# Flamingo block: the first chunk of x transposed ahead of its scale, Newton's step split between two engines, and GpSimd's order in the attention's last step

## The chip, the cores and the metric

The kernel runs on one core of one Trainium2 chip. A core has a matrix engine (TensorE, PE in the profile), a vector engine (VectorE, DVE), a scalar engine (ScalarE, ACT), GpSimd (POOL), and SyncE (SP), which only issues DMAs here. The metric is device time in microseconds, the median of several executions.

## The reference

Eight sequences of 256 rows of 256 numbers pass through a gated cross-attention with 16 heads and a gated feed-forward network whose activations and weights are rounded to 8 bits:

```python
x = x + tanh(g_xattn) * xattn(layernorm(x), ctx, ctx, Wq, Wk, Wv, Wo, bo, masks)
x = x + tanh(g_ffn) * ffn(layernorm(x), clip_x, clip_down, w_gate, w_up, w_down)

def act_fake_quant(x, clip):            # one scale for the whole tensor
    scale = sigmoid(clip) * max(abs(x)) / 127
    return clip_to_8_bits(round(x / scale)) * scale

def ffn(x, ...):
    xq = act_fake_quant(x, clip_x)
    h = act_fake_quant(silu(xq @ q(w_gate).T) * (xq @ q(w_up).T), clip_down)
    return h @ q(w_down).T
```

Two layer norms need a mean and 1/sqrt(variance + 1e-5) of each row. The scale of xq needs the largest magnitude of the whole normalised tensor, so no product of the feed-forward can begin before the last row is normalised.

## The kernel before

A batch is one sequence: 256 rows, two tiles of 128 partitions. There are B = 8 batches, 16 tiles, and every engine has a program of its own; semaphores order them. Each engine does its instructions in the order in which they are written.

**Projections.** For each batch VectorE takes row statistics (`stats`, L915 and L919), GpSimd turns the variance into 1/sqrt (`project_rstd`, `rstd`, L499 to L506), VectorE normalises (`normalise`, L925), TensorE transposes x and the context (`x_tr`, L1303 and L1309), ScalarE and VectorE copy the transposes, and TensorE projects (L1345, L1356). q and k are split into three bf16 parts by ScalarE (L702, L711), VectorE (L940) and GpSimd (`lo_parts`, L516); SyncE stores them in DRAM (L435) and loads them back stacked. The part buffers are two, by the batch's parity: batch 2's first parts wait until batch 0's have landed. SyncE's queue is one list: `ctx_load` of batch b (L352) waits until TensorE has transposed the context of batch b - 2; behind `ctx_load(3)` stand the loads of the feed-forward weights and the small inputs, and behind those the store of batch 0's parts.

**1/sqrt.** `rstd` is six operations of GpSimd over two columns: add epsilon (L499), raise to the power -0.5 (L500), and one Newton step in four operations (L501 to L506), which mends the rough power. Before the first of them GpSimd writes two rows of ones into k_st with a memset of 4096 words on two partitions (L492) and waits for it.

**Attention.** A step works on batch b while the maxima of batch b + 1 are taken. GpSimd's part of a step: the split of the maxima, the hats of an earlier batch (`hat`, L563 and L567: the second layer norm, written into v_all), head scales, `residual` (L576), `add_bias` (L589), `second_rstd`. VectorE takes the statistics of the second norm (L1070, L1078) and the row maxima of the hats (`row_maxima`, L1083). After the last step GpSimd works off what is left: residuals, one `rstd` over four columns for batches 4 and 5 at once (`newton_two`), the hats of batches 4 and 5, `second_rstd` and `hat` of batch 6, and `second_rstd` of batch 7. VectorE's `last_step` closes with the row maxima of batch 6, the residual of batch 7 (L1064) and its statistics; `last_row_maxima` (L1090, L1093) subtracts the mean of batch 7 and takes its maxima, and ScalarE multiplies these rows by rs2 (L850).

**From the attention to the feed-forward.** VectorE multiplies batch 7's maxima by rs2 (L1185), reduces, TensorE spreads the maximum over the partitions (L1545), VectorE makes the scale (L1189 to L1191). x comes in four chunks of 512 rows. For chunk 0, VectorE and ScalarE each scale half of it to int8 (L1203, L882), VectorE casts both halves to bf16 (L1195), TensorE transposes each half (L1573), ScalarE copies the transposes (L858), and TensorE multiplies, half by half (`first_product`, L1591). Chunks 1 to 3 are scaled by VectorE (1) and GpSimd (2 and 3, `over_scale`, L648, after a wait for the casts of chunk 0), cast by VectorE, and transposed between products. GpSimd's memset L643 pads h_all before that. wd_scale and PALL come from a product and a spread of TensorE (L1549, L1545) that VectorE reads.

Of the kernel before, what the change touches and what calls it, by code (L numbers as in the profile page):

```python
# [21 lines left out]
P = 128  # L22
# [43 lines left out]
def flamingo_block(nc, x, ctx_in, mask_rows, mask_full, g_xattn, g_ffn, Wq, Wk, Wv, Wo, bo,  # L66
# [60 lines left out]
    with ExitStack() as stack:  # L127
# [38 lines left out]
        minus_half = sb("minus_half", [P, 2, QC])  # L166
        newton_two = sb("newton_two", [P, 3, 2, QC])
        stats2 = sb("stats2", [P, QC, 6])
        mv2_now = sb("mv2_now", [P, 2, QC, 2])
        rs2 = sb("rs2", [P, NT])  # L170
        row_max = sb("row_max", [P, NT])
# [49 lines left out]
        x_int = part(NCH * CT * E // 4, True).bitcast(I8).rearrange("p (a t e) -> p a t e", a=NCH, t=CT)  # L221
        xq_b = part(NCH * CT * E // 2).bitcast(BF16).rearrange("p (a t e) -> p a t e", a=NCH, t=CT)
# [60 lines left out]
        poison_sum, x_over_scale, last_hat = sem("poison_sum"), sem("x_over_scale"), sem("last_hat")  # L283
        xq_ready, xq_tr, xq_t_ready = sem("xq_ready"), sem("xq_tr"), sem("xq_t_ready")
# [194 lines left out]
        def _(pool):  # L479
# [7 lines left out]
            chain.step(pool.memset(minus_half[:].rearrange("p a c -> p (a c)"), -0.5))  # L487
# [4 lines left out]
            pool.memset(k_st[KR:KM].rearrange("r a h s -> r (a h s)").bitcast(mybir.dt.uint32), 0x3F803F80  # L492
                        ).then_inc(ones_rows, 1)
            pool.wait_ge(ones_rows, 1)

            def rstd(y, var, v, t, out, half=minus_half[:, 0]):
# [3 lines left out]
                chain.step(pool.tensor_tensor(y, v, half, ALU.pow))  # L500
# [5 lines left out]
                return pool.tensor_tensor(out, y, t, ALU.mult)  # L506

# [15 lines left out]
            for b in range(3):  # L523
                project_rstd(b, b % 2)
# [109 lines left out]
            rstd(newton_two[:, 2], mv2_now[:, :, :, 1], newton_two[:, 0], newton_two[:, 1],  # L634
                 rs2[:, QC * (B - 4):QC * (B - 2)].rearrange("p (a c) -> p a c", a=2), minus_half[:]).then_inc(rs2_ready, 2)
# [17 lines left out]
            pool.wait_ge(xq_ready, 2)  # L653
# [19 lines left out]
        def _(act):  # L673
# [170 lines left out]

            act.activation(scal[:, 21:22], magic[:], ACT.Silu)
# [8 lines left out]
            def first_xq_copy(half):  # L854

                act.wait_ge(xq_tr, half + 1)
                cols = slice(half * 2 * P, (half + 1) * 2 * P)
                act.activation(xq_t[:, :, cols], spare[half][:].bitcast(BF16).rearrange("p (k t) -> p k t", k=EC)[:, :, cols],  # L858
                               ACT.Copy).then_inc(xq_t_ready, 1)

            def xq_copy(n):
                act.wait_ge(xq_tr, n + 2)
# [37 lines left out]
        def _(dve):  # L900
# [9 lines left out]
            def stats(b, p, j):  # L910
# [9 lines left out]
                done.then_inc(stats_done, 1)  # L920

# [49 lines left out]
            stats(0, 0, 0)  # L971
            normalise(0, 0)
# [205 lines left out]
            dve.wait_ge(diag_done, 1)  # L1178
            chain.step(dve.tensor_reduce(PALL, bank_o[:, E:E + P], axis=AX.X, op=ALU.add))
            chain.then(dve.tensor_tensor(SIG[:, 0:1], SIG[:, 0:1], PALL, ALU.add))  # L1180
            dve.tensor_copy(wd_scale[:], bank_o[:, 0:E]).then_inc(wd_scale_ready, 1)
            dve.wait_ge(rs2_ready, B + 1)
            dve.wait_ge(row_done, B)
# [490 lines left out]
```

## Time and profile before

| | us |
|---|---|
| median of 3 runs | 248.92 (248.47 to 249.05) |
| the profiled execution | 250.41 |
| its span | 248.8 |
| PE busy | 210.6 (85%) |
| DVE busy | 207.0 (83%) |
| ACT busy | 160.5 (64%) |
| POOL busy | 133.3 (54%) |

The span counts from the first to the last instruction; 1.6 us lie around it. A busy share is an average over stages with different limits. What a change is worth is read in its own stage: which wait ends last there. A timeline row merges neighbouring instructions of one kind (x2 is two of them) and closes with the idle time before it and what ended that. Line numbers are those of the kernel before.

### The profile page before, as it was taken

Reading aid. Unit: us, or ns where it says so; the run is one execution under the profiler, and the core shown is the slowest. Engines: PE = TensorE matmul, PEld = TensorE weight load, DVE = VectorE, ACT = ScalarE, POOL = GpSimd, SP = SyncE. Lnnn points to the kernel's source line nnn. Section 1 sums busy time; section 2 is a strip of 40 time slices with the busy share of each in tenths; the row PEclk is TensorE's granted clock in tenths of the full one; section 3 lists DMA queues with packets and bytes.
Section 4 is the critical chain, followed back from the end, with each engine's and each line's share of the span. In section 5 each row is a group of like instructions: output and inputs, shape, how many; then the busy total and the mean of one; then the engine's idle time right before and its main releaser. Section 6 shows DMA issues by size and latency. Waiting matters only on the chain.

```text
span 248.8 us, 5433 instructions
## 1 busy us (share of the span) xinstructions
PE 210.6 (85%) x1712; PEld 146.9 (59%) x1712; DVE 207.0 (83%) x417; ACT 160.5 (64%) x296; POOL 133.3 (54%) x235
## 2 busy tenths in 40 slices
PE   6699979979979999999999999989834989846940
PEld 6578868858746676666676767656422433314830
DVE  3388888978898998989999999964977689998990
ACT  2255487466597777787887776767624688838900
POOL 7446567642462343577585948437846444320880
PEclk9999999999999999999999999999995799995996
DMA  6989889999646553555555342000004200000594
GB/s 219 271 224 307 267 259 235 268 242 247 162 128 147 129 137 105 130 128 130 128 114 125 88 120 73 1 4 0 3 1 133 78 0 1 3 1 0 59 148 139
DMA packets 34186, 30.82 MB, mean 124 GB/s; under 512 B 5232, under 2 KB 27760, under 8 KB 34160
## 3 DMA queue, kind: packets, MB, share of 16 engines
q1 hardware_dynamic: 29776, 27.74, 41.5%
q0 software_dynamic: 1360, 1.31, 4.5%
q10 hardware_dynamic: 3024, 1.44, 2.1%
q8 instruction: 14, 0.23, 0.4%
q14 instruction: 12, 0.10, 0.1%
HBM read 20.65 MB, written 9.70 MB: 122 GB/s over the span
## 4 chain that ended last, share of the span: by engine, by line
PE 46%; DVE 18%; ACT 10%; issue 9%; POOL 7%; DMA 4%; SPq 3%; ACTq 0%; POOLq 0%; DVEq 0%
PE bank_o L1468 10%; PE bank_a L1451 9%; PE bank_b L1437 7%; PE bank_a L1345 6%; PE bank_a L1477 5%; ACT arena L795 4%; DMA qk_parts<-arena 3%; DVE h_max L1220 3%; DVE big L1229 2%; DVE arena L1257 2%; PE bank_o L1356 2%; DVE v_all L1263 2%; POOL big L492 1%; PE bank_a L1318 1%; DVE x_rows L1279 1%
## 5 line engine op out<-in xcount | busy, mean ns | idle before, releaser
L935 DVE TENSOR_REDUCE neg_max<-bank_b 128x2 f32<-128x512 f32 x128 | 80.2, 676 | 4.7 <-PE bank_b L1334 3.0
L1451 PE MATMUL bank_a<-big 98*128 98x256 bf16 x256 | 48.9, 273 | 3.9 <-ACT arena L795 2.3
L1437 PE MATMUL bank_b<-big 96*128 96x256 bf16 x224 | 42.7, 272 | 0.2 <-issue 0.2
L795 ACT ACTIVATE arena<-bank_a 128x512 f32<-128x512 f32 x64 | 34.2, 606 | 9.8 <-PE bank_a L1451 9.8
L795 ACT ACTIVATE big<-bank_a 128x512 f32<-128x512 f32 x64 | 33.7, 598 | 9.4 <-PE bank_a L1451 9.2
L1451 PEld LDWEIGHTS bank_a<-big 98*128 98x128 bf16 x256 | 20.9, 97 | 20.4 <-issue 7.7
L1345 PE MATMUL bank_a<-arena,w_t 128*128 128x256 f32 x128 | 30.2, 381 | 1.9 <-DVE resid L940 1.3
L1345 PEld LDWEIGHTS bank_a<-arena,w_t 128*128 128x128 f32 x128 | 23.2, 190 | 5.2 <-issue 2.5
L516 POOL TENSOR_TENSOR arena<-resid,arena 128x512 bf16<-128x512 f32 x16 | 18.2, 1156 | 10.9 <-ACT arena L711 10.9
L1437 PEld LDWEIGHTS bank_b<-big 96*128 96x128 bf16 x224 | 21.2, 97 | 4.2 <-DVE neg_max L935 0.8
L873 ACT ACTIVATE arena<-bank_b,w_scale_x 128x512 f32<-128x512 f32 (+1 forms) x24 | 16.1, 686 | 5.8 <-PE bank_b L1606 1.9
L576 POOL TENSOR_TENSOR x_rows<-x_rows,arena 128x256 f32<-128x256 f32 x14 | 10.2, 726 | 18.0 <-ACT arena L804 18.0
L660 POOL TENSOR_TENSOR big<-arena 128x512 f32<-128x512 f32 x8 | 10.1, 1266 | 17.1 <-ACT arena L877 17.1
L1606 PE MATMUL bank_b<-arena,wgu_t 128*128 128x512 bf16 (+1 forms) x60 | 17.1, 397 | 2.6 <-DVE big L1229 2.6
L702 ACT ACTIVATE arena<-bank_a 128x512 bf16<-128x512 f32 x16 | 9.4, 595 | 13.9 <-PE bank_a L1345 9.6
L1468 PE MATMUL bank_o<-arena,v_cur 128*32 128x256 f32 x256 | 15.7, 382 | 1.1 <-DVE arena L1032 1.1
L1032 DVE STREAM_TRANSPOSE arena<-bank_o 128x512 f32<-128x512 f32 (+1 forms) x17 | 11.6, 681 | 6.0 <-PE bank_o L1468 5.9
L550 POOL CAST max_parts<-max_f 8x256 bf16<-8x256 f32 x16 | 6.2, 387 | 17.5 <-issue 15.1
L1356 PE MATMUL bank_o<-w_t,arena 128*128 128x256 f32 x64 | 15.6, 381 | 0.0
L1468 PE MATMUL bank_o<-big,v_cur 128*32 128x256 f32 x256 | 15.5, 382 | 0.0
L1220 DVE TENSOR_REDUCE h_max<-big 128x1 f32<-128x512 f32 (+1 forms) x24 | 15.2, 670 | 0.0
L1477 PE MATMUL bank_a<-w_t,arena 128*128 128x256 f32 x56 | 14.4, 379 | 0.0
(185 smaller groups left out, 432.9 us busy)
## 6 DMA issues: line engine op xcount, KB each, us to landing
qk_parts<-arena SPq DMA_DIRECT2D x8, 768.0 KB, 5.0
big<-qk_parts SPq DMA_DIRECT2D x32, 192.0 KB, 3.3
big<-qk_parts SPq DMA_DIRECT2D x32, 128.0 KB, 3.3
x_rows<-in_x SPq DMA_DIRECT2D x8, 256.0 KB, 5.3
big<-qk_parts SPq DMA_DIRECT2D x32, 64.0 KB, 3.6
big<-in_ctx SPq DMA_DIRECT2D x7, 256.0 KB, 5.2
out<-x_rows SPq DMA_DIRECT2D x7, 256.0 KB, 3.0
out<-v_all POOLq DMA_DIRECT2D x5, 256.0 KB, 6.3
```

The source lines that it names most:

```text
L516: pool.tensor_tensor(parts[:, p, w, LO[w]], resid[:, p, w], parts[:, p, w, MID[w]], ALU.subtract).then_inc(lo_done, 1)
L795: act.activation(probabilities(h), ring_bank(b, ("exp", h)).rearrange("p (c s) -> p c s", c=QC), ACT.Exp, scale=SCALE).then_inc(exp_done, 1)
L873: act.activation(silu[0:r, c % 3], bank_b[0:r, c % 3], ACT.Silu, scale=w_scale_x[0:r, c:c + 1]).then_inc(silu_done, 1)
L935: dve.tensor_reduce(neg_max[:, p, :, h], bank.rearrange("p (c s) -> p c s", c=QC), axis=AX.X, op=ALU.max, negate=True).then_inc(max_done, 1)
L1220: chain.then(dve.tensor_reduce(h_max[0:r, tile(u)], h_all[0:r, c, bass.ds(n * CW, CW)], axis=AX.X, op=ALU.max, apply_absolute_value=True))
L1345: last = mm(bank_a[:, w, f * S:(f + 1) * S], w_t[:, w, k, f * P:(f + 1) * P], src[:, p, k * S:(k + 1) * S], start=(k == 0), stop=(k == EC ...
L1356: last = mm(bank_o[:, c * E:(c + 1) * E], ctx_t[:, p, k * S + c * P:k * S + (c + 1) * P], w_t[:, 2, k], start=(k == 0), stop=(k == EC - 1))
L1437: done = mm(to, q_st[0:KR, p, h, c * P:(c + 1) * P], k_st[0:KR, p, h], start=True, stop=not masked)
L1451: done = mm(to, k_st[0:KM, p, h, k * P:(k + 1) * P], q_st[0:KM, p, h], start=True, stop=not masked)
L1468: done = mm(bank_o[n * 2 * D:(n + 1) * 2 * D, g % 2 * S:(g % 2 + 1) * S], v_cur[:, p, k, h], probabilities(h)[:, k], start=(k == 0), stop= ...
L1477: done = mm(to[:, 0:E], att_t[:, p, f, c * P:(c + 1) * P], w_t[:, 3, f], start=(f == 0), stop=(f == EC - 1))
L1606: last = mm(to, wgu_t[:, g, k, c * P:c * P + r], xq_t[:, k, bass.ds(n * CW, CW)], start=(k == 0), stop=(k == EC - 1))
```

## The change

Three parts. (1) `rough_root`: for the first batch's x and for the last batch's second norm, GpSimd does only the add and the power; VectorE does the Newton step in three operations (`root`). GpSimd's memset of the rows of ones moves behind the first batch's power. (2) In the attention's last step GpSimd adds the bias first, the step over four columns becomes two single ones, and one of them comes ahead of the residuals of batch 6. TensorE computes the down projection's scales between the two halves of the last output projection. (3) The fp32 hats of chunk 0 are transposed ahead, while the scale is not known, and copied by ScalarE into hat_t; afterwards the scale and the cast are applied to the transposed rows and written straight into the operand of the product. ScalarE copies wd_scale instead of VectorE, and GpSimd's wait for the casts of chunk 0 goes.

```diff
-            pool.memset(k_st[KR:KM]...bitcast(uint32), 0x3F803F80).then_inc(ones_rows, 1)
-            pool.wait_ge(ones_rows, 1)
...
+            def rough_root(var):
+                alone(pool)
+                chain.step(pool.tensor_scalar(rough[:, 0], var, EPS, None, ALU.add))
+                pool.tensor_tensor(rough[:, 1], rough[:, 0], minus_half[:], ALU.pow).then_inc(rough_done, 1)
...
-            for b in range(3):
+            pool.wait_ge(stats_done, 1)
+            rough_root(mv1[:, 0, :, 1])
+            pool.wait_ge(rough_done, 1)
+            pool.memset(k_st[KR:KM]...bitcast(uint32), 0x3F803F80).then_inc(ones_rows, 1)
+            pool.wait_ge(ones_rows, 1)
+            for b in range(1, 3):
                 project_rstd(b, b % 2)
...
+            add_bias(B - 1)
             residual(B - 3, 1)
-            add_bias(B - 1)
+            second_rstd(B - 4, 0)
             residual(B - 2, 0)
             residual(B - 2, 1)
-            pool.wait_ge(means_done, B - 2)
-            alone(pool)
-            rstd(newton_two[:, 2], mv2_now[:, :, :, 1], ...).then_inc(rs2_ready, 2)
             hat(B - 4, 0)
+            second_rstd(B - 3, 1)
             hat(B - 3, 1)
             second_rstd(B - 2, 0)
             hat(B - 2, 0)
-            second_rstd(B - 1, 1)
+            pool.wait_ge(means_done, B)
+            rough_root(mv2_now[:, 1, :, 1])
             pool.wait_ge(rs2_ready, B + 1)
...
             pool.wait_ge(last_hat, 1)
-            pool.wait_ge(xq_ready, 2)
             over_scale(2)
...
+            act.wait_ge(diag_done, 1)
+            act.activation(wd_scale[:], bank_o[:, 0:E], ACT.Copy).then_inc(wd_scale_ready, 1)
+            for f in range(EC):
+                act.wait_ge(hat_tr, f + 1)
+                act.activation(hat_t[:, f], bank_a[:, f], ACT.Copy).then_inc(hat_t_ready, 1)
...
-            act.activation(x_int[:, 0, 2:4], v_all[:, 2:4], ACT.Copy, scale=INV_X).then_inc(x_over_scale, 1)
-            first_xq_copy(0)
-            first_xq_copy(1)
+            act.wait_ge(hat_t_ready, EC)
+            act.activation(first_int[:, :, 2 * P:], hat_t[:, :, 2 * P:], ACT.Copy, scale=INV_X).then_inc(x_over_scale, 1)
+            act.wait_ge(x_over_scale, 1)
+            act.activation(xq_t[:, :, 2 * P:CW], first_int[:, :, 2 * P:], ACT.Copy).then_inc(xq_t_ready, 1)
+            act.wait_ge(scale_ready, 2)
...
+            def root(n, out, done):
+                dve.wait_ge(rough_done, n)
+                chain.step(dve.scalar_tensor_tensor(rough[:, 2], rough[:, 1], -0.5, rough[:, 0], ALU.mult, ALU.mult))
+                chain.step(dve.scalar_tensor_tensor(rough[:, 3], rough[:, 2], 1.0, rough[:, 1], ALU.mult, ALU.mult))
+                dve.scalar_tensor_tensor(out, rough[:, 3], 1.5, rough[:, 1], ALU.add, ALU.mult).then_inc(done, 1)
...
             stats(0, 0, 0)
+            root(1, rs1[:, 0], rstd_done)
             normalise(0, 0)
...
+            root(2, rs2[:, last], rs2_ready)
             dve.wait_ge(rs2_ready, B + 1)
             dve.wait_ge(row_done, B)
...
-            chain.step(dve.tensor_scalar(x_int[:, 0, 0:2], v_all[:, 0:2], INV_X, None, ALU.mult))
-            whole_x(0, slice(0, 2))
-            chain.step(dve.tensor_scalar(w_scale_x[:], w_scale[:, 0:2 * IC], S_X, None, ALU.mult))
-            dve.wait_ge(x_over_scale, 1)
-            whole_x(0, slice(2, 4))
+            dve.wait_ge(hat_t_ready, EC)
+            chain.step(dve.tensor_scalar(first_int[:, :, 0:2 * P], hat_t[:, :, 0:2 * P], INV_X, None, ALU.mult))
+            dve.tensor_copy(xq_t[:, :, 0:2 * P], first_int[:, :, 0:2 * P]).then_inc(xq_first, 1)
+            dve.tensor_scalar(w_scale_x[:], w_scale[:, 0:2 * IC], S_X, None, ALU.mult).then_inc(scale_ready, 1)
+            dve.wait_ge(scale_ready, 2)
...
                 for f in range(EC):
                     pe.wait_ge(at_done, 2 * B - 1 + f)
+                    if f:
+                        pe.wait_ge(hat_done, 3)
+                        pe.wait_ge(out_scaled_done, QC * (B - 1))
...
+                    if f == 0:
+                        weight_scales()
...
+                for f in range(EC):
+                    for t in range(CT):
+                        done = tr(bank_a[:, f, t * P:(t + 1) * P], v_all[:, t, f * P:(f + 1) * P], ident_f[:])
+                    done.then_inc(hat_tr, 1)
...
-                first_xq_transpose(0)
-                first_xq_transpose(1)
...
-                        pe.wait_ge(xq_t_ready, half + 1)
+                        pe.wait_ge(*((xq_first, 1), (xq_t_ready, 1))[half])
```

## Rows read from the trace of the kernel before

**Rows 1.** Chain that ended last, 0 to 35 us: start us, us, what.
```profile
2.52 3.52 POOL big L492
...
16.30 1.38 SPq L387
...
23.62 7.54 DMA qk_parts<-arena
```

**Rows 2.** Timeline, 0 to 24 us: start, us, engine, line, operation, [idle before <-releaser].
```profile
5.54 0.25 DVE L919 BATCH_NORM_AGGREGATE mv<-stats 128x2 f32<-128x6 f32 x2
...
6.60 0.72 POOL L500 TENSOR_TENSOR rs<-newton,minus_half 128x2 f32<-128x2 f32 x1
...
8.67 0.74 DVE L925 TENSOR_SCALAR arena<-x_rows,mv,rs 128x256 f32<-128x256 f32 x2 [2.88 <-POOL rs L506]
...
9.46 0.66 PE L1303 MATMUL bank_b<-ident_f,arena 128*128 128x128 f32 x4 [1.88 <-DVE arena L925]
```

**Rows 3.** Timeline, 23.5 to 42 us, ScalarE.
```profile
31.24 1.08 ACT L702 ACTIVATE arena<-bank_a 128x512 bf16<-128x512 f32 x2 [3.69 <-DMA qk_parts<-arena]
```

**Rows 4.** Timeline, 0 to 24 us, GpSimd and VectorE at once.
```profile
19.99 2.27 POOL L516 TENSOR_TENSOR arena<-resid,arena 128x512 bf16<-128x512 f32 x2
...
21.04 1.70 DVE L925 TENSOR_SCALAR arena<-x_rows,mv,rs 128x256 f32<-128x256 f32 x2
```

**Rows 5.** Timeline, 160 to 200 us: the attention's last step.
```profile
170.83 0.72 POOL L576 TENSOR_TENSOR x_rows<-x_rows,arena 128x256 f32<-128x256 f32 x1 [1.20 <-ACT arena L804]
...
172.74 0.29 POOL L499 TENSOR_SCALAR newton_two<-mv_now 128x4 f32<-128x4 f32 x1
...
178.55 0.23 POOL L499 TENSOR_SCALAR newton<-mv_now 128x2 f32<-128x2 f32 x1
...
181.15 1.10 POOL L567 TENSOR_SCALAR v_all<-x_rows,minus_mean,rs 128x256 f32<-128x256 f32 x2
...
182.28 0.69 DVE L1083 TENSOR_REDUCE row_max<-v_all 128x2 f32<-128x512 f32 x1 [1.15 <-POOL v_all L567]
...
182.47 0.70 PE L1549 MATMUL bank_o<-wd_diag,ones_f 128*128 128x256 f32 x2
```

**Rows 6.** Timeline, 160 to 200 us: from batch 7's statistics to the first product.
```profile
184.82 0.25 DVE L1078 BATCH_NORM_AGGREGATE mv_now<-stats 128x2 f32<-128x6 f32 x2 [0.18 <-DVE stats L1070]
...
185.34 0.22 POOL L499 TENSOR_SCALAR newton<-mv_now 128x2 f32<-128x2 f32 x1 [3.10 <-DVE mv_now L1078]
...
185.75 0.69 DVE L1093 TENSOR_REDUCE row_max<-v_all 128x2 f32<-128x512 f32 x1
...
187.70 0.16 DVE L1185 TENSOR_TENSOR row_max<-row_max,rs 128x2 f32<-128x2 f32 x1 [0.54 <-POOL rs L506]
...
187.73 1.80 POOL L643 MEMSET big<- 64x2048 f32 x1
...
189.47 0.49 DVE L1203 TENSOR_SCALAR arena<-v_all,scal 128x512 int8<-128x512 f32 x1
...
189.99 0.43 DVE L1195 CAST arena<-arena 128x512 bf16<-128x512 int8 x1
...
191.23 2.96 POOL L648 TENSOR_SCALAR arena<-v_all,scal 128x1024 int8<-128x1024 f32 x2 [1.71 <-DVE arena L1195]
191.72 1.50 DVE L1195 CAST arena<-arena 128x1024 bf16<-128x1024 int8 x1
...
191.93 1.86 PE L1591 MATMUL bank_b<-arena,wgu_t 128*128 128x256 bf16 x8 [0.24 <-ACT arena L858]
```

**Rows 7.** Chain that ended last, 180 to 200 us: pairs of 512-column matmuls.
```profile
194.64 0.85 PE bank_a L1606 x2
...
197.22 0.45 PE bank_b L1606 x2
```

**Rows 8.** Stretches of 1 us: length, PE busy, granted clock, DMA share, GB/s.
```profile
185.00:186.00 1.00, 0.00 (x0) 0.98 0.00 0
...
196.00:197.00 1.00, 1.00 (x11) 0.90 0.00 0
```

More of the change, by code:

```diff
@@ L165, in flamingo_block @@
         minus_mean = sb("minus_mean", [P, 2, QC])
-        minus_half = sb("minus_half", [P, 2, QC])
-        newton_two = sb("newton_two", [P, 3, 2, QC])
+        minus_half = sb("minus_half", [P, QC])
         stats2 = sb("stats2", [P, QC, 6])
@@ L170, in flamingo_block @@
         rs2 = sb("rs2", [P, NT])
+        rough = sb("rough", [P, 4, QC])
+        hat_t = sb("hat_t", [P, EC, CW])
         row_max = sb("row_max", [P, NT])
@@ L486, in _ @@
                                    pattern=[[-1, P]], channel_multiplier=1).then_inc(idents, 1)
-            chain.step(pool.memset(minus_half[:].rearrange("p a c -> p (a c)"), -0.5))
+            chain.step(pool.memset(minus_half[:], -0.5))
             pool.sem_inc(rs2_ready, 1)
@@ L491, in _, with rstd @@
             pool.wait_ge(pad_zero, 1)
-            pool.memset(k_st[KR:KM].rearrange("r a h s -> r (a h s)").bitcast(mybir.dt.uint32), 0x3F803F80
-                        ).then_inc(ones_rows, 1)
-            pool.wait_ge(ones_rows, 1)
-            def rstd(y, var, v, t, out, half=minus_half[:, 0]):
+            def rstd(y, var, v, t, out):
                 alone(pool)
                 chain.step(pool.tensor_scalar(v, var, EPS, None, ALU.add))
-                chain.step(pool.tensor_tensor(y, v, half, ALU.pow))
+                chain.step(pool.tensor_tensor(y, v, minus_half[:], ALU.pow))
                 chain.step(pool.tensor_tensor(t, v, y, ALU.mult))
@@ L521, in project @@
                 lo_parts(b, p)
-            for b in range(3):
+            pool.wait_ge(stats_done, 1)
+            rough_root(mv1[:, 0, :, 1])
+            pool.wait_ge(rough_done, 1)
+            pool.memset(k_st[KR:KM].rearrange("r a h s -> r (a h s)").bitcast(mybir.dt.uint32), 0x3F803F80
+                        ).then_inc(ones_rows, 1)
+            pool.wait_ge(ones_rows, 1)
+            for b in range(1, 3):
                 project_rstd(b, b % 2)
@@ L852, in _ @@
             act.wait_ge(scale_ready, 1)
[L854 to L859, printed above, removed]
             def xq_copy(n):
-                act.wait_ge(xq_tr, n + 2)
+                act.wait_ge(xq_tr, n)
                 act.activation(xq_t[:, :, bass.ds(n * CW, CW)],
@@ L1174, in _ @@
             last_row_maxima()
-            dve.wait_ge(diag_done, 1)
+            last = slice((B - 1) * QC, B * QC)
+            root(2, rs2[:, last], rs2_ready)
+            dve.wait_ge(rs2_ready, B + 1)
+            dve.wait_ge(row_done, B)
+            chain.step(dve.tensor_tensor(row_max[:, last], row_max[:, last], rs2[:, last], ALU.mult))
+            dve.tensor_reduce(TMP, row_max[:], axis=AX.X, op=ALU.max).then_inc(amax_part, 1)
+            dve.wait_ge(wd_scale_ready, 1)
             chain.step(dve.tensor_reduce(PALL, bank_o[:, E:E + P], axis=AX.X, op=ALU.add))
             chain.then(dve.tensor_tensor(SIG[:, 0:1], SIG[:, 0:1], PALL, ALU.add))
-            dve.tensor_copy(wd_scale[:], bank_o[:, 0:E]).then_inc(wd_scale_ready, 1)
-            dve.wait_ge(rs2_ready, B + 1)
-            dve.wait_ge(row_done, B)
-            last = slice((B - 1) * QC, B * QC)
-            chain.step(dve.tensor_tensor(row_max[:, last], row_max[:, last], rs2[:, last], ALU.mult))
-            dve.tensor_reduce(TMP, row_max[:], axis=AX.X, op=ALU.max).then_inc(amax_part, 1)
             dve.wait_ge(amax_spread, 1)
@@ L1536, in attend, with spread, weight_scales @@
                             done.then_inc(wo_done, 1)
+                    if f == 0:
+                        weight_scales()
                 ffn_weights(9)
                 feed_forward()
-            def feed_forward():
-                def spread(to, column):
-                    return tr(to, column.to_broadcast([P, P]), ident_f[:])
+            def spread(to, column):
+                return tr(to, column.to_broadcast([P, P]), ident_f[:])
+            def weight_scales():
+                pe.wait_ge(turn_done, 2 * B + 1)
                 pe.wait_ge(diag_ready, 1)
@@ L1565, in xq_transpose @@
                     done.then_inc(xq_tr, 1)
-                def first_xq_transpose(half):
-                    pe.wait_ge(xq_ready, half + 1)
-                    bank = spare[half][:].bitcast(BF16)
-                    for k in range(EC):
-                        for t in range(2 * half, 2 * half + 2):
-                            done = tr(bank[:, k * CW + t * P:k * CW + (t + 1) * P], xq_b[:, 0, t, k * P:(k + 1) * P],
-                                      ident_b[:])
-                    done.then_inc(xq_tr, 1)
-                first_xq_transpose(0)
-                first_xq_transpose(1)
                 up_banks = (bank_b[:, 3], bank_a[:, 0], bank_a[:, 1])
@@ L1596, in gate_up @@
                 def gate_up(n, first=0, ahead=True):
-                    pe.wait_ge(xq_t_ready, n + 2)
+                    pe.wait_ge(xq_t_ready, n + 1)
                     for c in range(first, IC):
```

8 lines of the change are left out of this document (4 added, 4 removed).

## The prediction

> **What bounds the kernel now.** I read the chain of work that ended last, then the timeline at the two places that the diff touches, then the granted clock there. In the first 31 us the chain runs through GpSimd's memset of 4096 words (2.52 to 6.03), Newton's step for batch 0, TensorE's first transposes, and then SyncE: its queue issues a DMA every half microsecond or so without a gap until batch 0's parts leave at 23.62; they land at 31.16 [rows 1]. ScalarE has then stood 3.69 us waiting for them [rows 3], so what the SP queue does is the bound there and the compute engines have slack. From there the chain is that of the attention, which the diff leaves alone until its last step. There it runs through GpSimd: the double Newton step (172.74), two hats, one single step (178.55) and hat 6, which ends at 182.25; VectorE waited 1.15 us for it [rows 5]. The gap to the feed-forward is one serial chain: statistics (end 185.07), GpSimd's six Newton operations, VectorE's use of them at 187.70, the scale at 189.47, int8, bf16, transposes, ScalarE's copy, and the first product at 191.93 [rows 6].
>
> **Part 1, the start.** Now: statistics at 5.79 (5.54 + 0.25), memset until 6.03, Newton's step, normalise at 8.67, transposes at 9.46 [rows 1, 2]. Changed: GpSimd starts some 0.2 us after the statistics, adds and raises to the power: 5.99 + 0.24 + 0.08 + 0.72 = 7.03 [rows 2, 6]. VectorE's three small operations are not in the trace; the nearest are 0.16 for two columns [rows 6] and 0.25 for two small aggregates [rows 2]; with their waits 0.6 to 0.75 in all, I take 0.7. So normalise could start at 7.75, 0.9 us earlier.
>
> But the memset now starts at 7.03 + 0.05 and runs 3.51 us, until 10.59, across normalise. The trace has no GpSimd memset beside this VectorE operation. It has another GpSimd operation beside it: at 21.04 normalise starts while GpSimd's L516 pair runs until 22.26 (19.99 + 2.27) [rows 4]. The pair of halves takes 1.70 us instead of the 0.74 of batch 0 [rows 2]; the second is its usual 0.33 long, so the first ends at 22.41, 0.15 us after GpSimd does. VectorE stood until GpSimd had ended. If a memset does the same, normalise ends at 10.59 + 0.15 + 0.33 = 11.07 and the transposes start at 11.12 instead of 9.46: 1.66 us late. Bounds for this edit: 0.9 us gained to 1.66 lost; I take the loss, as the only row in which this operation meets a GpSimd operation shows a full stop. The Trainium skill (SBUF — State Buffer, Who interferes with whom) has the rule that a VectorE operation in a 2-port mode and any GpSimd instruction exclude each other for the whole instruction; by it the loss is 1.66 too, and its half that this trace shows (rows 4) agrees, though no row here shows it for a memset.
>
> What is queued behind: on VectorE the statistics of batch 1 and so GpSimd's second Newton step, all late by the same; batch 1's rows still come before TensorE is through with batch 0's products, so it is batch 0 that counts. SyncE waits for the transposes of batches 0 and 1 (ctx_load), then issues its eleven DMAs. One of them, 16.30, takes 1.38 us where its neighbours take some 0.4 to 0.6 [rows 1]; a later start may shorten that stall by up to 1.0. So the parts leave, and land, 0.66 to 1.66 late; I take **+1.3**. Nothing later gives it back, because ScalarE's wait for this landing only has slack on its other side.
>
> Second, TensorE. Before, it idles 1.88 us ahead of the transposes, from 7.58 [rows 2]; held, it idles 3.5 us. The granted clock fell to the 1.2 GHz level at about 186.0 [rows 8], some 2.7 us after the matmuls that ended near 183.3 [rows 5], and came back to 2.4 GHz at about 196.2, 4.2 us after the first product began [rows 6, 8]. An idle of 3.5 us is longer than that 2.7. If the clock falls, some 4 us of matmuls run at half speed: 0.85 us a pair against 0.45 [rows 7], so up to 1.9 us lost ahead of batch 1's transposes, for which SyncE waits. Bounds 0 and 1.9; since 3.5 us is near the 2.7 at which it fell, I count it in about half of the executions: **+1.0**.
>
> **Part 2, attention's last step.** add_bias moves ahead of a residual that waits for ScalarE anyway; in its place a single Newton step for batch 4 (2.3 us, as at 178.55) fills GpSimd up to residual 6,0 at 170.83, ahead of which it stood 1.20 us. Both residuals still end by 172.65. Then hat 4 (1.37 us), and twice Newton's step with a hat (178.55 to 182.25 = 3.70 each with 0.08 ahead): 172.74 + 1.37 + 3.78 + 3.78 = 181.67 instead of 182.25 [rows 5]: **-0.58**. What is late next: VectorE's turns and TensorE's last projection. The weight scales (0.70 and a spread of 0.3) [rows 5] now lie between its two halves and push the second from 181.18 to about 181.4; its first column block is done near 182.0, before VectorE needs it at 182.35. Cover 0.3 us; were it gone, this term would be worth that much less.
>
> **Part 3, the last Newton step.** Now: statistics end to use, 185.07 to 187.70 = 2.63. Changed: GpSimd 0.27 + 0.22 + 0.09 + 0.71 = 1.29, but VectorE is busy with row maxima until 186.44 = 1.37 [rows 6]; then 0.7: 2.1. **-0.53**.
>
> **Part 4, scale to first product.** U is VectorE's use of rs2. Now the scaling starts at U + 1.77 and the product at U + 4.23. Changed: scaling 0.49, cast 0.43 straight into the operand, 0.15 to TensorE: U + 2.87, which is 1.36 earlier [rows 6]. ScalarE's half (about 0.7 + 0.6) is ready at about U + 3.3 and hides behind TensorE's first half, 0.93 [rows 6]. The eight fp32 transposes and two copies of 0.6 fill idle time; ScalarE's list (wd_scale, two copies, the table load) grows by 1.6 us and still ends just ahead of its next wait, for rs2. But GpSimd no longer waits for the casts. Its padding memset starts when rs2 is there and ends at about U + 2.0 (1.80 long), and its scaling of chunk 2 follows at once, at about U + 2.15, while VectorE's cast starts at U + 2.29. The trace shows this pair: the cast at 191.72 beside L648 took 1.50 us, a cast of half the size alone 0.43 [rows 6]. If GpSimd comes first, the cast waits 1.0 to 1.48 us, and of the 1.36 between 0 and 0.5 is left. It is a matter of 0.15 us, so I take the middle: **-0.9**, bounds -1.36 and 0.
>
> **Clock after the product.** Without the transposes ahead of it the product is the first work, so the low level lasts somewhat longer past it: 0 to 0.9, I take **+0.3**. (A pair costs 0.40 more at the low level [rows 7], and VectorE's work hides part.)
>
> **Edits at nothing.** The order of PALL behind amax_part lies in the 0.6 us in which TensorE spreads the maximum. The scaling of chunks 2 and 3 on GpSimd starts 2 us earlier, which nobody needs. SyncE's and GpSimd's DMAs are the same ones, released by the same semaphores.
>
> **Sum.** 1.3 + 1.0 - 0.58 - 0.53 - 0.9 + 0.3 = +0.6 us. The profiled execution has a span of 248.8 and a time of 250.41; the median of the runs is 248.92, 1.5 less. So a span of 249.4, a profiled time of 251.0 and a median of **249.5**. Its own bounds: 0.66 - 1.11 - 1.36 = -1.8 to 1.66 + 1.9 - 1.11 + 0.9 = +3.35; within it 248.3 to 251.2 is the likely stretch.
>
> **Rivals.**
> - *The memset doesn't hold VectorE.* For: no row shows a memset holding it. Against: [rows 4]. Then the start gains 0 to 0.9 (the SP stall may eat it), I take 0.6, and the rest is -1.7: 246.6. This is the other side; it decides by one thing, whether normalise 0 lasts 0.4 or about 3 us. Chance 0.17.
> - *It holds, but TensorE's clock stays up at the start*, or GpSimd loses the race for the cast: without the 1.0, or with 0.5 more in part 4: -0.4 to -0.9, 248.3. For: 3.5 us is not much over 2.7. Chance 0.25.
> - *The memset holds Newton's three operations as well.* They would run from 10.59, normalise ends 0.95 us later still: 250.7. Nearest row: 0.16 us for such an operation that starts 0.03 before a memset [rows 6], which settles nothing. Chance 0.06. The same section of the Trainium skill says that a VectorE operation with two SBUF inputs is stopped only by a GpSimd instruction that reads SBUF, which a memset doesn't; by it this rival falls. No row here shows it.
> - *The change doesn't do what it says*: the transposes of the hats are late and part 4 brings nothing: about 250.4. They need only hats 0 to 3, long done. Chance 0.02.
>
> **Chances.** Forecast 0.50 (slower 0.42, same 0.08), first rival 0.17 (faster), second 0.25 (faster 0.12, same 0.11, slower 0.02), third and fourth 0.08 (slower). Together: faster 0.29, same 0.19, slower 0.52, where same is within 0.2%, 0.5 us, about what a measurement of this kernel can tell. The range runs from the first rival's 246.6 to 251.1, with a tenth at most left out above.
>
> **What would show it.** At the start: GpSimd's 3.5 us memset from about 7.1; normalise 0 ends at 11.1 (forecast) or at 8.5 (first rival); granted clock below full between 8 and 16; SyncE's parts DMA at 24.3 or later instead of 23.62. In the last step hat 6 ends 0.6 us earlier against its neighbours; 2.1 us from statistics to use; 2.9 us (cast first) or 3.8 (GpSimd first) from use to product. I am wrong if normalise 0 isn't held, or if SyncE's chain of DMAs absorbs the delay.

## The result, and the profile after

| | before | after |
|---|---|---|
| median, us (20 runs each, taken together) | 248.39 (247.53 to 250.14) | 250.24 (249.07 to 252.85) |
| ratio | 1 | 1.0066 [1.0045, 1.0087] |
| the profiled execution | 250.41 | 251.27 |
| its span | 248.8 | 249.7 |

The kernel became slower, by 0.66%. The ratio is that of the fast runs, and one of the 20 of after (252.85) was a slow one; 0.66% of 248.4 is 1.6 us, while the medians differ by 1.85. The forecast was 249.5 with slower as the likeliest sign; 250.24 lies in its range, and the forecast was too small by 0.7 us, or, measured as a difference (+0.6 against +1.6), by 1.0.

The page of after: the first lines of busy time, then the slices of 6.2 us with the granted clock.

```profile
span 249.7 us, 5433 instructions
PE 211.0 (85%) x1709; PEld 148.7 (60%) x1712; DVE 209.8 (84%) x421; ACT 161.3 (65%) x298; POOL 132.5 (53%) x233
...
PEclk9979999999999999999999999999997799995995
```

VectorE is busy 2.8 us longer than before; the pair of normalise 0 alone is 2.7 longer, as the next rows show. The 7 in the third slice of PEclk is new; before, the clock is full there. The timeline of after from 6 to 35 us:

```profile
7.09 0.16 DVE L935 SCALAR_TENSOR_TENSOR rough<-rough 128x2 f32<-128x2 f32 x1 [1.28 <-POOL rough L512]
7.11 3.51 POOL L532 MEMSET big<- 2x4096 uint32 x1
7.28 0.16 DVE L936 SCALAR_TENSOR_TENSOR rough<-rough 128x2 f32<-128x2 f32 x1
...
7.48 0.16 DVE L937 SCALAR_TENSOR_TENSOR rs<-rough 128x2 f32<-128x2 f32 x1
...
7.67 3.41 DVE L942 TENSOR_SCALAR arena<-x_rows,mv,rs 128x256 f32<-128x256 f32 x2
...
11.14 0.66 PE L1321 MATMUL bank_b<-ident_f,arena 128*128 128x128 f32 x4 [3.52 <-DVE arena L942]
...
12.53 5.38 PE L1363 MATMUL bank_a<-arena,w_t 128*128 128x256 f32 x16 [0.30 <-issue]
...
19.67 0.47 SPq L390 DMA_DIRECT2D x_rows<-in_x  x1
...
26.17 0.40 SPq L438 DMA_DIRECT2D qk_parts<-arena  x1
...
33.90 1.08 ACT L712 ACTIVATE arena<-bank_a 128x512 bf16<-128x512 f32 x2 [4.09 <-DMA qk_parts<-arena]
```

Line 942 is the normalise of L925 before, now 3.41 us instead of 0.74 [rows 2]: it ends at 11.08, 0.46 after the memset (7.11 + 3.51 = 10.62). The transposes start at 11.14 instead of 9.46. The sixteen matmuls of batch 0's q and k take 5.38 us, in the kernel before 3.69 (such a row stands with experiment 1). The x load at 19.67 takes 0.47 where it took 1.38 [rows 1]. The parts leave 2.55 us late (26.17 against 23.62) and ScalarE is released 2.66 late (33.90 against 31.24, [rows 3]). Stretches of 1 us of after: length, busy time of PE, PEld, DVE, ACT, POOL, granted clock, DMA share, GB/s.

```profile
11.00:12.00 1.00, 0.86 (x8) 0.86 (x8) 0.85 (x5) 0.17 (x1) 0.00 (x0) 1.00 0.45 131
12.00:13.00 1.00, 0.70 (x4) 0.50 (x2) 0.83 (x3) 0.43 (x1) 0.59 (x2) 0.77 0.00 0
13.00:14.00 1.00, 1.00 (x4) 0.73 (x3) 0.00 (x0) 0.00 (x0) 0.74 (x3) 0.50 0.56 111
15.00:16.00 1.00, 1.00 (x3) 0.80 (x3) 1.00 (x4) 0.00 (x0) 0.00 (x0) 0.52 0.52 149
16.00:17.00 1.00, 1.00 (x6) 0.88 (x5) 0.43 (x4) 0.60 (x1) 0.24 (x2) 1.00 0.91 280
```

TensorE had stood 3.52 us ahead of the transposes, and its clock is at the 1.2 GHz level (0.50) from 12.54 to 15.95, across those matmuls.

The attention carries this unchanged: its first exponential comes 2.65 us late (72.14 against 69.49), its last residual of batch 6 ends 2.70 late (175.35 against 172.65). From there, the timeline of after, to hat 6 and its maxima:

```profile
182.32 0.19 POOL L504 TENSOR_SCALAR newton<-newton 128x2 f32<-128x2 f32 x1 [0.20 <-POOL newton L502]
...
182.74 0.20 DVE L1058 RECIPROCAL rec<-arena 128x8 f32<-128x8 f32 x1
...
182.97 0.29 DVE L1062 TENSOR_TENSOR arena<-arena,rec 128x128 f32<-128x128 f32 x1
182.99 0.33 POOL L506 TENSOR_TENSOR rs<-newton 128x2 f32<-128x2 f32 x1 [0.48 <-POOL newton L504]
...
183.58 1.10 POOL L579 TENSOR_SCALAR v_all<-x_rows,minus_mean,rs 128x256 f32<-128x256 f32 x2
...
184.71 0.69 DVE L1101 TENSOR_REDUCE row_max<-v_all 128x2 f32<-128x512 f32 x1 [0.97 <-POOL v_all L579]
```

Hat 6 ends at 184.68, 9.33 after that residual; before it was 9.60 [rows 5]. On the same timeline, from batch 7's statistics to the first product:

```profile
187.25 0.25 DVE L1096 BATCH_NORM_AGGREGATE mv_now<-stats 128x2 f32<-128x6 f32 x2 [0.17 <-DVE stats L1088]
...
188.05 0.71 POOL L512 TENSOR_TENSOR rough<-rough,minus_half 128x2 f32<-128x2 f32 x1
...
188.79 0.16 DVE L935 SCALAR_TENSOR_TENSOR rough<-rough 128x2 f32<-128x2 f32 x1
...
189.37 0.16 DVE L1200 TENSOR_TENSOR row_max<-row_max,rs 128x2 f32<-128x2 f32 x1
189.40 1.80 POOL L654 MEMSET big<- 64x2048 f32 x1 [0.65 <-DVE rs L937]
...
191.00 0.49 DVE L1222 TENSOR_SCALAR arena<-hat_t,scal 128x512 int8<-128x512 f32 x1
191.30 2.43 POOL L659 TENSOR_SCALAR arena<-v_all,scal 128x1024 int8<-128x1024 f32 x2
191.53 1.23 DVE L1223 CAST arena<-arena 128x512 bf16<-128x512 int8 x1
...
192.90 1.87 PE L1608 MATMUL bank_b<-arena,wgu_t 128*128 128x256 bf16 x8 [2.71 <-DVE arena L1223]
```

Statistics end to use is 189.37 - 187.50 = 1.87 (before 2.63). Use to product is 192.90 - 189.37 = 3.53 (before 4.23): GpSimd's scaling of chunk 2 started 0.23 ahead of the cast, and the cast took 1.23 us instead of 0.43. The product starts 0.97 late (192.90 against 191.93, [rows 6]). The sum: +2.70 up to the last residual (+2.66 at the landing), -0.27 in part 2, -0.76 in part 3, -0.70 in part 4. The last addition of the kernel is 0.83 late, the span 0.9 longer.

### The profile page after: what moved, and what is told of

Read it like the earlier page. It is cut to its first block, busy times and chain, and to the rows that moved or that the text cites. A ratio compares the mean times of both kernels' runs of the same rounds, so it can differ in the third digit from the quotient of the medians.

```text
span 249.7 us, 5433 instructions
## 1 busy us (share of the span) xinstructions
PE 211.0 (85%) x1709; PEld 148.7 (60%) x1712; DVE 209.8 (84%) x421; ACT 161.3 (65%) x298; POOL 132.5 (53%) x233
## 4 chain that ended last, share of the span: by engine, by line
PE 46%; DVE 20%; issue 10%; ACT 9%; DMA 5%; POOL 4%; SPq 3%; ACTq 0%; POOLq 0%; DVEq 0%
PE bank_o L1486 10%; PE bank_a L1469 9%; PE bank_b L1455 7%; PE bank_a L1363 7%; PE bank_a L1495 5%; ACT arena L805 4%; DMA qk_parts<-arena 3%; DVE h_max L1238 3%; DVE big L1247 2%; DVE arena L1275 2%; PE bank_o L1374 2%; DVE v_all L1281 2%; DMA x_rows<-in_x 1%; PE bank_a L1336 1%; DVE x_rows L1297 1%
## 5 line engine op out<-in xcount | busy, mean ns | idle before, releaser
L1363 PE MATMUL bank_a<-arena,w_t 128*128 128x256 f32 x128 | 31.9, 397 | 1.9 <-DVE resid L957 1.3
L1363 PEld LDWEIGHTS bank_a<-arena,w_t 128*128 128x128 f32 x128 | 24.4, 200 | 5.7 <-issue 2.5
L1623 PE MATMUL bank_b<-arena,wgu_t 128*128 128x512 bf16 (+1 forms) x57 | 16.1, 391 | 3.1 <-DVE big L1247 2.9
```

What stands on the lines that cost most here:

```text
L1363: last = mm(bank_a[:, w, f * S:(f + 1) * S], w_t[:, w, k, f * P:(f + 1) * P], src[:, p, k * S:(k + 1) * S], start=(k == 0), stop=(k == EC ...
L1623: last = mm(to, wgu_t[:, g, k, c * P:c * P + r], xq_t[:, k, bass.ds(n * CW, CW)], start=(k == 0), stop=(k == EC - 1))
```

## The experiments

A difference below about 0.4% between two of these kernels is within their intervals. All ratios are to the kernel before, run on the same chip at the same time.

**1. Is it the memset?** The memset of the rows of ones goes back to its old place, all else stays changed.

```diff
+            pool.memset(k_st[KR:KM]...bitcast(uint32), 0x3F803F80).then_inc(ones_rows, 1)
+            pool.wait_ge(ones_rows, 1)
...
             rough_root(mv1[:, 0, :, 1])
             pool.wait_ge(rough_done, 1)
-            pool.memset(k_st[KR:KM]...bitcast(uint32), 0x3F803F80).then_inc(ones_rows, 1)
-            pool.wait_ge(ones_rows, 1)
```

> The changed kernel with GpSimd's memset of the rows of ones back at its old place, ahead of batch 0's power; all else as changed. Theory (the memset holds VectorE's normalise 0, and the idle that follows lets TensorE's clock fall): normalise 0 takes 0.74 us for its pair instead of 3.41 and starts near 7.9, TensorE's first transposes start near 8.7, the clock stays full until the attention's end, the store of batch 0's parts is issued at 23.0 to 23.6 instead of 26.17. The time falls by 2.5 to 3.2 us against the changed kernel, to about 1.2 us under the kernel before (ratio about 0.995). Rival (the loss lies at the end: the low clock beside the first products, or the changed order): the start looks as said but the time stays over the kernel before, ratio 1.003 or more.

Measured: 245.42 us, ratio 0.9891 [0.9857, 0.9925]. Its timeline, the start:

```profile
7.94 0.73 DVE L942 TENSOR_SCALAR arena<-x_rows,mv,rs 128x256 f32<-128x256 f32 x2
...
10.12 3.69 PE L1363 MATMUL bank_a<-arena,w_t 128*128 128x256 f32 x16 [0.30 <-issue]
...
22.71 0.40 SPq L438 DMA_DIRECT2D qk_parts<-arena  x1
```

Normalise is back at 0.73, the matmuls at 3.69, and the parts leave 3.46 us earlier than in after. Of these, 2.41 are the hold of normalise (11.08 against 8.67) and 1.69 the clock, less 0.64 that SyncE's queue gives back. The parts also landed 0.73 us faster (7.00 instead of 7.73), so the first exponential comes 4.33 us earlier (67.81 against 72.14), and the ratio is lower by 1.75%, 4.3 us. With experiment 5's wait in both kernels (runs e2 and e3, below) the same move gives 3.36 us at the first exponential and 1.1%, 2.8 us. So one instruction in another place is worth some 3 to 4 us, and with it back the rest of the change is a gain of 1.1%. That is more than was expected of this run (2.5 to 3.2 us against the changed kernel, ratio 0.995), and its parts left at 22.71, earlier than the 23.0 expected at best.

**2. The clock apart from the hold.** The memset stays late, but TensorE multiplies on through its wait: 70 unread matmuls instead of 8.

```diff
-            unread(8)
+            unread(70)
```

> The changed kernel with 62 more 128-column bf16 matmuls, read by nobody, in TensorE's idle time before the first transposes, so that its clock has no reason to fall there; normalise 0 is still held. Theory (of the 2.5 us lost at the start about 1.7 in this execution is the clock): the 16 matmuls of batch 0's q and k take 3.7 us instead of 5.4, the granted clock stays at the 2.4 GHz level, the store of batch 0's parts is issued near 24.6 instead of 26.17, and the time falls by about 1 us against the changed kernel on average (0.7 to 1.6). Rival (the clock costs nothing, SyncE's queue being bound by the DMAs): the store is issued at 26 as before and the time stays.

Measured: 248.45 us, ratio 0.9982 [0.9955, 1.0009], so 0.84% below after. Its timeline:

```profile
7.69 3.41 DVE L942 TENSOR_SCALAR arena<-x_rows,mv,rs 128x256 f32<-128x256 f32 x2
...
12.55 3.69 PE L1363 MATMUL bank_a<-arena,w_t 128*128 128x256 f32 x16 [0.30 <-issue]
...
24.79 0.40 SPq L438 DMA_DIRECT2D qk_parts<-arena  x1
...
33.53 1.08 ACT L712 ACTIVATE arena<-bank_a 128x512 bf16<-128x512 f32 x2 [4.33 <-DMA qk_parts<-arena]
```

The hold is the same 3.41, the clock stays at 1.00 in each stretch from 11 to 15 us, and the matmuls take 3.69. So the clock's part is real and is worth up to 1.69 us of TensorE and 1.38 in SyncE's queue. In this profiled execution only 0.37 of that reached ScalarE, since the parts took 8.74 us to land instead of 7.73; the ratios differ by 2.1 us (0.7 to 1.6 was expected). Why the landing varies was not found. The parts left 1.17 us later than in the kernel before (24.79 against 23.62), so at the issue of the parts the hold alone costs 1.17 us and the clock another 1.38.

The mean granted clock of each run says how often the clock fell: 3.4 us at half speed take some 0.007 off the mean of a 250 us run (an estimate from the rows above). In after it is 0.948 to 0.958 in all 20 runs, here 0.960 to 0.968 in eleven of twelve. Of e2's twelve, which start as after does, ten have 0.960 or less, and two 0.964 and 0.965. So, by this estimate, the clock fell in all runs of the changed kernel and in most of e2's.

**3. Part 1 alone**, on the kernel before, with the memset late as in the change.

```diff
-            pool.memset(k_st[KR:KM]...bitcast(uint32), 0x3F803F80).then_inc(ones_rows, 1)
-            pool.wait_ge(ones_rows, 1)
...
-            for b in range(3):
+            pool.wait_ge(stats_done, 1)
+            rough_root(mv1[:, 0, :, 1])
+            pool.wait_ge(rough_done, 1)
+            pool.memset(k_st[KR:KM]...bitcast(uint32), 0x3F803F80).then_inc(ones_rows, 1)
+            pool.wait_ge(ones_rows, 1)
+            for b in range(1, 3):
...
+            root(1, rs1[:, 0], rstd_done)
```

> The kernel before with the change's first part alone: rough power on GpSimd and Newton's step on VectorE for batch 0, the memset of the rows of ones behind the power. Theory (the whole loss is here, and the other two parts gain 1.7 us in the trace): normalise 0 ends near 11.1, and the time is 3 to 4 us over the kernel before, ratio 1.012 to 1.016, thus more than the whole change's 1.0066. Rival (the parts at the end lose as well, or gain nothing): ratio 1.007 or less.

Measured: 252.52 us against 249.41, ratio 1.0134 [1.0098, 1.0169]. Its timeline:

```profile
11.06 1.12 PE L1322 MATMUL bank_b<-ident_f,arena 128*128 128x128 f32 x4 [2.90 <-DVE arena L943]
...
12.91 4.23 PE L1364 MATMUL bank_a<-arena,w_t 128*128 128x256 f32 x16
```

The start alone costs 3.3 us by the ratio. Here the clock was already low when the transposes came (low from 10.59 to 14.01), so they pay too (1.12 instead of 0.66) and the matmuls pay less. The loss of part 1 is shown by doing it alone and by undoing it.

**4. How does the hold depend on the memset's length?** The rows of ones are written in two pieces, the first early, the second in the changed place: 2048 of 4096 words late (the rest as in the changed kernel), or 1024 late (with experiment 5's wait too), whose edit is shown.

```diff
+            pool.memset(k_st[KR:KM]...bitcast(uint32)[:, 0:3072], 0x3F803F80).then_inc(ones_rows, 1)
+            pool.wait_ge(ones_rows, 1)
...
-            pool.memset(k_st[KR:KM]...bitcast(uint32), 0x3F803F80).then_inc(ones_rows, 1)
-            pool.wait_ge(ones_rows, 1)
+            pool.memset(k_st[KR:KM]...bitcast(uint32)[:, 3072:4096], 0x3F803F80).then_inc(ones_rows, 1)
+            pool.wait_ge(ones_rows, 2)
```

> The changed kernel with half of the memset (2048 words, 1.8 us) at the old place and half behind batch 0's power. Held until the memset ends: normalise 0 ends at 7.1 + 1.8 + 0.15 + 0.33 = 9.4 (11.08 with 4096 words, 8.7 with none), TensorE's first transposes start at 9.4, the idle ahead of them is 1.8 us and the granted clock stays full. If the hold isn't set by the memset's end, another time.

> The kernel with both mends (memset early, GpSimd's scaling behind the cast), but the memset in two pieces: 3072 words at the old place, 1024 words behind batch 0's power. If a memset holds a running normalise until it ends and no longer, the late piece of 0.9 us (7.1 to 8.0) holds it for 0.3 us: normalise 0 ends at 8.0 + 0.15 + 0.33 = 8.5, against 8.66 with the whole memset early, since GpSimd's power comes 0.25 us earlier; no change in the time beyond 0.2 us, ratio 0.988. If a memset in this place costs more than its own length (a fixed penalty for the meeting), normalise 0 ends after 8.9.

Timeline of the kernel with half of it late, then of the one with a quarter late:

```profile
7.02 1.80 POOL L535 MEMSET big<- 2x2048 uint32 x1
...
7.58 1.70 DVE L945 TENSOR_SCALAR arena<-x_rows,mv,rs 128x256 f32<-128x256 f32 x2
```

```profile
7.22 0.95 POOL L535 MEMSET big<- 2x1024 uint32 x1
...
7.78 0.85 DVE L946 TENSOR_SCALAR arena<-x_rows,mv,rs 128x256 f32<-128x256 f32 x2
```

The memset ends at 10.62, 8.82 and 8.17 in the three lengths, and normalise at 11.08, 9.28 and 8.63: each time 0.46 later. Normalise doesn't slow down by a factor, it waits for the end. With half of it late the clock stayed up (matmuls 3.69) and its single run gave 246.60 us, 1.1% under the kernel before; with a quarter late 244.52, ratio 0.9805 [0.9768, 0.9842]. The latter is below the 0.988 expected; experiment 6 repeats it.

**5. The race for the cast.** GpSimd's scaling of chunk 2 waits for VectorE's cast, as it waited for both casts before the change; the memset stays late.

```diff
             pool.wait_ge(last_hat, 1)
+            pool.wait_ge(xq_first, 1)
             over_scale(2)
```

> The changed kernel with one wait put in: GpSimd scales chunk 2 only after VectorE's cast of the first half (xq_first). Theory (GpSimd's operation came first and held the cast): the cast takes 0.43 us instead of 1.23, w_scale_x 0.23 instead of 1.08, and the first product begins 2.7 to 2.9 us after VectorE's use of rs2 instead of 3.53; the time falls by 0.5 to 0.9 us against the changed kernel, ratio to the kernel before about 1.003. Rival (something else sets the first product, or the chunks that GpSimd scales later are missed afterwards): the product does not come earlier, or the gain is given back in the next 6 us, and the ratio stays at 1.006.

Measured: 248.93 us, ratio 0.9995 [0.9961, 1.0029]. Its timeline:

```profile
191.44 0.43 DVE L1224 CAST arena<-arena 128x512 bf16<-128x512 int8 x1
...
192.02 1.86 PE L1609 MATMUL bank_b<-arena,wgu_t 128*128 128x256 bf16 x8 [1.91 <-DVE arena L1224]
...
192.07 3.15 POOL L659 TENSOR_SCALAR arena<-v_all,scal 128x1024 int8<-128x1024 f32 x2 [1.10 <-DVE w_scale_x L1225]
```

The cast is 0.43 again and the product starts at use + 2.87 instead of + 3.53, exactly the forecast's figure for a cast that comes first. That makes 0.66; the ratio moved by 0.7% (1.8 us; 0.5 to 0.9 was expected). Another 0.4 us stand in this trace behind the product (50.21 to the end of the last addition against 50.62), where the low clock lasted 3.16 us instead of 3.96. That these 0.4 come from the wait isn't shown: two executions of one kernel with the wait (e3 and e9) differ by 0.6 in the same stretch. The rest is within the intervals.

**6. Both mends**, the early memset and the wait, twice, beside the split memset for the second time.

> Both edits of the two kernels before this one: memset at its old place, GpSimd's scaling behind the cast. If the two losses are separate, the gains add: 3.2 to 4 us under the changed kernel, about 2 us under the kernel before, ratio 0.990 to 0.993. If one hides the other, it is no better than the better of the two.

> The same kernel as e3_both once more, beside the split memset on the same chip. Theory (the two placements differ by nothing that can be measured, and the 0.8% between their first measurements is scatter between calls): ratio 0.985 to 0.988 here, within 0.3% of the split one. Rival (the split memset is better by a mechanism of its own): 0.5% or more over the split one again.

> The same kernel as e6_quarter_late once more. Theory: 0.983 to 0.988, as e9. Rival: 0.981 or less while e9 stays near 0.988.

Measured: 245.85 us, ratio 0.9882 [0.985, 0.9915]; again 244.95, 0.9843 [0.9791, 0.9895]; the split memset 245.04, 0.9822 [0.9777, 0.9868]. The split memset brings nothing that can be told from the whole one ahead. That both mends are better than the early memset alone (0.9891) isn't shown by the medians taken together with it (245.85 against 245.42), only by the trace: use to product 2.86 instead of 3.51. Its parts landed 0.77 us later in that execution, for the same start.

So there is a kernel that beats both: the changed one with the memset in its old place and the wait for the cast is 1.2 to 1.6% under the kernel before and, by the quotient of the ratios, 1.8 to 2.2% under the changed one.

**7. Parts 2 to 4 without part 1**, mended: batch 0's whole Newton step on GpSimd as before; and the same with GpSimd's old order in the last step, which leaves parts 3 and 4.

```diff
-            rough_root(mv1[:, 0, :, 1])
...
-            for b in range(1, 3):
+            for b in range(3):
...
-            root(1, rs1[:, 0], rstd_done)
```

> The kernel with both mends, but batch 0's Newton step all on GpSimd as before the change, so the start is that of the kernel before and parts 2 to 4 stand alone. Theory: normalise 0 ends at 9.4 as before; the start's gain of 0.7 us is gone and parts 2 to 4 give 2.3 to 2.6 us, ratio 0.990. Rival (the start's earlier Newton step brings nothing, the store of the parts landing when the DMAs let it): ratio as with both mends, 0.988.

> e8_newton0_gpsimd (both mends, batch 0's Newton step on GpSimd) with GpSimd's old order in the attention's last step, so that parts 3 and 4 stand alone. Theory: from the end of batch 6's last residual to the end of hat 6 it takes 9.6 us as in the kernel before, instead of 8.9; the first product begins 0.3 to 0.7 us later than in e8 against that residual; ratio 0.989 (e8: 0.9866). Rival (TensorE's inserted weight scales, not GpSimd, are last there): no difference from e8 in the time from that residual to batch 7's statistics.

Measured: 245.94 us, ratio 0.9866 [0.9832, 0.9899]; with the old order 246.36, 0.9899 [0.9854, 0.9944]. The first lies between the two measurements of the kernel with both mends (0.9882 and 0.9843): part 1, even with the memset early, has no gain that the ratios show, and the rival expectation (the earlier Newton step brings nothing) isn't excluded. In the traces batch 0's parts leave at 23.52 without it and at 22.94 and 22.97 with it, and the first exponential comes at 69.21 against 68.70 and 68.72. The ratios don't tell the two orders apart either. In the traces the residual of batch 6 to the end of hat 6 takes 8.89 us with the new order and 9.59 with the old (before 9.60): part 2 is worth 0.7 us here, where the changed kernel had 9.33. From hat 6 to the product is 7.56 in both, 9.68 before: parts 3 and 4 are worth 2.1. One thing differs between 8.89 and 9.33, in this timeline of the kernel with the new order:

```profile
179.72 0.19 POOL L509 TENSOR_TENSOR rs<-newton 128x2 f32<-128x2 f32 x1 [0.18 <-POOL newton L507]
179.78 0.20 DVE L1055 RECIPROCAL rec<-arena 128x8 f32<-128x8 f32 x1
```

Here GpSimd's last Newton operation started 0.06 ahead of VectorE's reciprocal. In after it was due at 182.69 (182.51 + 0.18), didn't start until 182.99, just after the reciprocal had ended (182.94), and then took 0.33 beside a VectorE operation over two SBUF tiles instead of 0.19. Of the ten profiled executions with the new order (after, e1 to e4 and e6 to e10), the four with a gap of 0.18 to 0.23 started it at most 0.03 after the reciprocal's start, and the six with a gap of 0.47 or 0.48 after its end. When it was due doesn't part them: that was 0.01 to 0.07 ahead of the reciprocal in all ten. No experiment moved the reciprocal, so this is a pattern in the rows, not a cause shown.

## Why the prediction held, and where it was off

**The memset holds normalise**: right. Forecast: memset at 7.08 to 10.59, normalise to 11.07, transposes at 11.12. Measured: 7.11 to 10.62, 11.08, 11.14. The step from another GpSimd operation [rows 4] to a memset was sound. By the Trainium skill (SBUF — State Buffer, Who interferes with whom) it is one lock for the whole instruction whatever GpSimd does in it. Here the trace agrees: the pair ends 0.46 us after the memset's end for three lengths.

**Rival 3, Newton's three operations held too**: fell. They ran at 7.09, 7.28 and 7.48 beside the memset, 0.16 us each. The same section of the Trainium skill says that an operation with two SBUF inputs isn't stopped by a GpSimd instruction that only writes; these rows agree. The rival's price was also added up wrongly: 0.95 us on 249.5 is 250.4, not 250.7.

**The first and the last rival** (the memset doesn't hold; the change brings nothing) fell with the rows above. Of the second, neither half came true in the changed kernel. GpSimd didn't lose the race for the cast, it won it. The clock stayed up only when TensorE was given work (e4) or half of the memset or less was late (e7, e6 and e10). The rival's price, -0.4 to -0.9, also needs the clock to stay up: a cast that comes first is worth 0.5, which alone leaves +0.1.

**The start, forecast +1.3 and +1.0, measured +2.66 at the landing.** The stall in SyncE's queue (1.38) shrank by 0.91, as its bound of 1.0 allowed, and the clock took 1.69 us of TensorE's time, of the 1.9 allowed. So transposes +1.68, matmuls +1.69, queue -0.91, and 0.1 of small ones: +2.55 for the parts. The mechanism was right and both terms were bounded rightly. Run e4 parts them at the issue of the store: 1.17 for the hold (forecast 1.3) and 1.38 for the clock (forecast 1.0). So it is the clock term that was too small, because I had it fall in half of the executions. It fell in the three profiled executions with the whole memset late and nothing to keep TensorE busy (after, e2 and e5), the mean granted clocks put it in nearly all runs (experiment 2), and undoing it (e4) moved the ratio by 2.1 us. The value to take was 1.4 or more.

**Part 2, forecast -0.58, measured -0.27.** The order by itself does more than forecast (-0.7 in the kernel without part 1), but in the changed kernel 0.30 of waiting and 0.14 of a longer operation stand in L506. The step that failed is "twice Newton's step with a hat", 3.78 each with the wait ahead: the first took 3.77 (176.71 to 180.48), the second 4.20 (to 184.68). A duration from one place was put in another, where VectorE's reciprocal falls at the same moment. The cover of 0.3 us for the weight scales held: VectorE's wait for hat 6 is still 0.97.

**Part 3, forecast -0.53, measured -0.76.** The three operations take 0.58 from the first to the use (188.79 to 189.37), not 0.7, and the wait before them was shorter: statistics end to the first of them 1.29, GpSimd's own chain, without the 0.08 that I had added for VectorE's maxima.

**Part 4, forecast -0.9, measured -0.70.** The end for a cast that comes first was right: use + 2.87 (run e2). The other end was too dear: GpSimd first holds the cast by 0.80 (1.23 against 0.43), not by 1.0 to 1.48, and the first of its two scalings took 1.2 us where L648 before took 1.5. The product came at use + 3.53, not 3.8, and 0.70 of the 1.36 was left, not 0 to 0.5. I took the middle of a race between the two ends; GpSimd won it in each of the four profiled executions of a kernel with the new cast and without the added wait (after, e1, e4 and e7: 1.23 each). The race wasn't as close as forecast: the rows before put the end of the padding memset at use + 1.83 (187.73 + 1.80 against 187.70), not 2.0, and GpSimd's scaling then started at use + 1.93, ahead of the cast at + 2.16. The middle of a race that falls the same way each time is a value that never occurs; that -0.9 came near -0.70 is luck. The scaling itself began at use + 1.63 rather than + 1.77, because the spread of the maximum took 0.31 instead of 0.45 at the clock's full level; it fell at 190.03, after it.

**The clock after the product, forecast +0.3, measured about 0**: low for 3.96 us after the product's start, before 4.27 (to 196.20). From the product to the last addition the two kernels take 50.62 and 50.76.

**The sum**: +0.97 at the product and +0.9 in the span by one execution each; the ratio says +1.6 and the medians +1.85. The two profiled executions stand unequally to their medians: 250.41 is 2.0 above that of the kernel before and above all of its 20 runs, 251.27 is 1.0 above that of after. So the difference of the two traces understates that of the medians by 1.0 us, and none of their stages shows the rest. How much one execution can be off is seen in runs with the same start code: e3 and e9 reach the first exponential 0.9 us later than e1. The forecast took 1.5 between profiled time and median, so the profiled time, 251.27 against 251.0, was hit more closely than the median. Term by term the traces are off by +0.4 (start), +0.3 (part 2), -0.2 (part 3), +0.2 (part 4) and -0.4 (clock at the end): that they nearly cancel is luck.

## What to carry to other kernels

Where an operation like VectorE's fp32 normalise or its cast from SBUF to SBUF is on the path, keep long GpSimd operations off it, even a memset of two partitions: move them to where VectorE reads PSUM or reduces, or ahead of the data's arrival. In this timeline of after, the copy out of PSUM and the reduction take their usual 0.69 and 1.21 beside GpSimd's pair:

```profile
21.74 2.28 POOL L522 TENSOR_TENSOR arena<-resid,arena 128x512 bf16<-128x512 f32 x2
...
21.99 0.69 DVE L948 COPY arena<-bank_b 128x512 f32<-128x512 f32 x1 [1.48 <-PE bank_b L1327]
...
22.60 1.21 DVE L975 TENSOR_REDUCE mask_sum<-mask_u 128x4 f32<-128x1024 uint8 x1
```

Price such a hold twice, once for its length and once for what a longer idle of TensorE does to its clock. A wait that looks needless may be what keeps two engines apart; before one is removed, ask which operations of the two engines it put in order, and when both start within tenths of a microsecond of each other, reckon with the bad order, as in the four executions here.

## What the runs showed of the hardware that I had not expected

- A hold ends 0.46 us after GpSimd's instruction, whatever its length (0.95, 1.80 or 3.51 us): 0.33 of it is the second half of the pair, so 0.13 passes until the first half is done.
- A hold of 2.4 us cost 3 to 4: the clock fell, after the first transposes (12.54) or during the wait (10.59 in the run of part 1 alone), and came back 3.4 us later (15.95 and 14.01).
- The time from the issue of the parts' store to ScalarE's release is 7.0 us in one execution and 8.7 in another (22.71 to 29.71, 24.79 to 33.53), and took back 1.01 of the 1.38 us that e4's earlier issue had gained.
- GpSimd's small operation over two columns came 0.3 us late, just after the end of a VectorE reciprocal of 0.20, in six of ten executions, though it was due 0.01 to 0.07 ahead of the reciprocal in all ten; that the reciprocal holds it is not shown.
